# Layer 2 of a four-layer gated model, rebuilt: exponential ahead of the clip, packed normalise, shorter output product, work shared out anew over VectorE, ScalarE, GpSimd and TensorE

## The reference, cut to what matters

```python
x = x + tanh(g_xattn[2]) * L2_xattn(layernorm(x), ctx, mask, ...)
x = x + tanh(g_ffn[2]) * L2_ffn(layernorm(x), w_gate, w_up, w_down)

# L2_xattn: 16 heads of 16 columns
q, k, v = proj(hs, Wq, bq), proj(at, Wk, bk), proj(at, Wv, bv)
scores = clip(einsum(q, k) / 4, -50, 50)
scores = clip(where(attend, scores, -10000.0), -50, 50)
probs = softmax(scores); probs = probs / (probs.sum(-1) + 1e-8)
delta = (probs @ v) @ Wo.T + bo
delta = clip(residual_scale, 0, 0.3) * delta
delta = (delta - mean) / sqrt(var + 1e-5) * ln_gamma + ln_beta

# L2_ffn: 832 hidden columns
weight_quant(w) = clip(round(w * s), -1, 1) / s           # s = 1 / mean|w|
act_quant(x)    = clip(round(x * s), -128, 127) / s       # s = 127 / max|x| of the row
bitlinear(x, w) = act_quant(x) @ weight_quant(w).T
y = bitlinear(silu(bitlinear(x, w_gate)) * bitlinear(x, w_up), w_down)
```

## Time and profile before

| | us |
|---|---|
| median of 3 runs | 2442.97 (2437.24 to 2443.68) |
| the profiled execution | 2458.33 |
| its span | 2456.8 |
| layer 2 in it: from 1261.34 to 1675.53 | 414.2 |
| VectorE busy in the span | 1617.9 (66%) |
| TensorE busy in the span | 1959.7 (80%) |

### The profile page before, as it was taken

The page is one execution under the profiler, slowest core; times in us unless marked ns, Lnnn a source line. Parts: engine busy times, 40 slices in busy tenths (PEclk is TensorE's granted clock), DMA queues, the critical chain, the costliest instruction groups (busy, mean ns, idle before and its releaser), DMA issues.

```text
span 2456.8 us, 35107 instructions
## 1 busy us (share of the span) xinstructions
PE 1959.7 (80%) x12408; PEld 1268.5 (52%) x12438; DVE 1617.9 (66%) x3820; ACT 900.5 (37%) x2036; POOL 526.9 (21%) x623
## 2 busy tenths in 40 slices
PE   6888899999976888787864655545699999987697
PEld 2444445555545667675233433323466666656344
DVE  8888744544358999998247777772356666655447
ACT  3666621111114656665122333321234334433232
POOL 3122100000012333332112222111013322332231
PEclk8999999999997999999886777776899999998869
DMA  4543120000014333331112332206100000000966
GB/s 96 155 99 67 39 84 0 1 1 0 1 23 91 77 72 72 77 75 32 46 30 78 91 88 59 52 1 224 60 1 29 29 14 6 1 1 1 249 194 259
DMA packets 160397, 158.03 MB, mean 64 GB/s; under 512 B 84424, under 2 KB 139088, under 8 KB 156288
## 3 DMA queue, kind: packets, MB, share of 16 engines
q1 hardware_dynamic: 150912, 146.31, 22.4%
q0 software_dynamic: 6144, 8.82, 1.1%
q10 hardware_dynamic: 3168, 0.66, 0.1%
HBM read 103.27 MB, written 60.82 MB: 67 GB/s over the span
## 4 chain that ended last, share of the span: by engine, by line
PE 53%; DVE 31%; issue 8%; ACT 5%; DMA 2%; POOL 1%; SPq 0%; ACTq 0%; another core or an unknown queue 0%; DVEq 0%; POOLq 0%
PE psum L983 10%; PE psum L1003 5%; PE psum L2857 4%; PE psum L2783 4%; DVE sbuf L534 3%; PE psum L381 3%; PE psum L1891 2%; DVE sbuf L1539 2%; PE psum L2850 2%; DVE sbuf L1546 2%; PE psum L2832 2%; PE psum L344 2%; PE psum L2819 1%; DVE sbuf L2348 1%; PE psum L3348 1%
## 5 line engine op out<-in xcount | busy, mean ns | idle before, releaser
L983 PE MATMUL psum<-sbuf 128*128 128x512 f32 (+1 forms) x544 | 246.7, 596 | 0.0
L181 POOL TENSOR_TENSOR sbuf<-sbuf 128x1 f32<-128x1 f32 x128 | 73.9, 580 | 747.7 <-DVE sbuf L173 747.1
L534 DVE TENSOR_REDUCE sbuf<-psum 128x2 f32<-128x512 f32 x256 | 164.8, 685 | 30.5 <-PE psum L344 29.4
L3170 ACT ACTIVATE sbuf<-psum,sbuf 128x128 f32<-128x128 f32 x256 | 113.8, 454 | 188.2 <-DVE sbuf L3005 182.2
L1677 ACT ACTIVATE sbuf<-psum 128x512 f32<-128x512 f32 x256 | 139.9, 597 | 107.5 <-PE psum L1403 94.3
L1109 DVE SCALAR_TENSOR_TENSOR sbuf<-sbuf,psum 128x512 f32<-128x512 f32 (+1 forms) x68 | 46.8, 688 | 196.8 <-ACT sbuf L1172 196.8
L983 PEld LDWEIGHTS psum<-sbuf 128*128 128x128 f32 (+1 forms) x544 | 100.4, 188 | 106.6 <-issue 104.2
L1172 ACT ACTIVATE sbuf<-psum 128x512 f32<-128x512 f32 (+1 forms) x68 | 40.7, 598 | 310.0 <-PE psum L983 310.0
L681 ACT ACTIVATE sbuf<-psum 128x1024 f32<-128x1024 f32 x128 | 130.7, 1023 | 41.5 <-PE psum L366 34.5
L1003 PE MATMUL psum<-sbuf 128*128 128x256 f32 (+1 forms) x544 | 129.2, 380 | 0.7 <-DVE sbuf L1114 0.7
L2783 PE MATMUL psum<-sbuf 128*128 128x256 f32 x512 | 123.0, 396 | 3.4 <-DVE sbuf L2963 1.9
(11 more groups left out here) (388 smaller groups left out, 4555.7 us busy)
## 6 DMA issues: line engine op xcount, KB each, us to landing
l_pair_outputs<-sbuf SPq DMA_DIRECT2D x24, 512.0 KB, 6.9
sbuf<-in_l_gu_pairs SPq DMA_DIRECT2D x32, 384.0 KB, 8.9
sbuf<-l_pair_outputs SPq DMA_DIRECT2D x16, 768.0 KB, 15.1
sbuf<-l_q_parts SPq DMA_DIRECT2D x16, 384.0 KB
l_q_parts<-sbuf SPq DMA_DIRECT2D x64, 96.0 KB, 2.0
sbuf<-l_q_parts SPq DMA_DIRECT2D x32, 192.0 KB
l_k_parts<-sbuf SPq DMA_DIRECT2D x64, 96.0 KB, 2.0
sbuf<-l_k_parts SPq DMA_DIRECT2D x32, 192.0 KB
```

The costliest lines, as they stand in the source:

```text
L534: dve.tensor_reduce(top3[:, 2 * hp:2 * hp + 2, c], score_bank[v % 2].rearrange("p (j t) -> p j t", j=2), AXX, ALU.max, negate=True).then_i ...
L983: last = pe.matmul(up_bank[v % 2][0:M, n * BANK:(n + 1) * BANK], wn[:, k, fs], xt_t[blk % 2][:, k, :], start=(k == 0), stop=(k == KD - 1))
L3170: last = act.activation(e_t[u % 3][:, j * P:(j + 1) * P], score_bank[:, j * P:(j + 1) * P], ACT.Exp, bias=mt[:, j:j + 1], scale=rq[:, lo + ...
```

## The change

Attention. `act_exp` now reads the scores from PSUM and writes SBUF, and `dve_clip` clips the exponentials in place, in SBUF, between exp(50) and exp(-50). `dve_normalise` writes only the 16 used columns of each head (128 in place of 256), so its second turn, the stored tile and Wo halve: `pe_project_out` has two products, and a third one of a single row (ones times `row`), which brings in both biases: `row` is bv through Wo plus bo, made once by `pe_bias_row`. Wo is scaled by the residual scale once, gamma and beta by the gate, all in `act_scale_weights`. The sums of the norm are taken from PSUM (`dve_delta_stats`), `dve_add_attention` is two instructions, and beta is added to x ahead, by `pool_add_beta`. The bias of keys and queries and the copy of values move from VectorE to ScalarE (`act_bias`, `act_values`), and the norm ahead of the queries to GpSimd (`pool_norm`).

Feed-forward. The mean is taken off on ScalarE (`act_less_mean`), 1/sqrt(var) enters only as a factor of the scale, the rounded values are turned as fp32 (`m.ident` in place of `m.ident_bf`) and lose ROUND in the copy out of PSUM, so `act_xq` and `act_hq` go. Three scales of a block move to GpSimd (`pool_scales`, `pool_out_scale`). `hq_bank` is now banks 6 and 7, `down_bank` 5.

The loop has 19 passes (NB + 3): attention of block i, whose second half is weighed and normalised in pass i + 1, norm and quantising of block y = i - 2, gate and down product of block f = i - 3. The order in each pass is new on all engines. The clearing of Wo (L2020, a memset on VectorE at the start of layer 1's feed-forward part) goes.

```diff
     def load(self):
-        dve.wait_ge(*self.m.x_l1a.at(NB))
-        dve.memset(self.wo, 0.0).then_inc(*self.cleared.up())
...
     def pe_project_out(b):
         pe.wait_ge(*normed.at(2 * b + 2))
-        for j in range(4):
-            last = pe.matmul(av_bank[:, 0:D], attn_t[b % 2][:, j * P:(j + 1) * P], w.wo[:, j, :], start=(j == 0), stop=(j == 3))
+        pe.wait_ge(*av_read.at(min(2 * b + 3, 2 * NB)))
...
+        pe.matmul(av_bank[:, 0:D], ones[0:1, :], row, start=True, stop=False)
+        for s in range(2):
+            last = pe.matmul(av_bank[:, 0:D], attn_t[b % 2][:, s * P:(s + 1) * P], w.wo[:, s, :], start=False, stop=(s == 1))
...
-        dve.tensor_scalar(d_t[u % 4], score_bank, 50.0, -50.0, ALU.min, ALU.max).then_inc(*clipped.up())
+        dve.wait_ge(*exped.at(u + 1))
+        dve.tensor_scalar(d_t[u % 4], d_t[u % 4], EXP_HIGH, EXP_LOW, ALU.min, ALU.max).then_inc(*clipped.up())
...
-        dve.tensor_tensor(T3, T3, R.unsqueeze(2).broadcast_to([P, 8, 32]), ALU.mult).then_inc(*m.chain.up())
+        dve.tensor_tensor(packed.rearrange("p (c j r) -> p j c r", j=2, r=HD2), T3[:, :, :, 0:HD2],
+                          R.rearrange("p (j c) -> p j c", j=2).unsqueeze(3).broadcast_to([P, 2, 4, HD2]), ALU.mult).then_inc(*m.chain.up())
...
     def dve_add_attention(b):
+        dve.scalar_tensor_tensor(d, av_bank[:, 0:D], s[:, 6:7], w.gamma, ALU.subtract, ALU.mult).then_inc(*y_read.up())
+        dve.wait_ge(*y_rstd.at(b + 1))
+        dve.wait_ge(*beta_added.at(b + 1))
+        dve.wait_ge(*y_read.at(b + 1))
+        dve.scalar_tensor_tensor(m.X[b], d, s[:, 8:9], m.X[b], ALU.mult, ALU.add).then_inc(*x_mid.up())
...
+    def act_less_mean(f):
+        act.wait_ge(*f_var.at(f + 1))
...
+        act.activation(n_t[f % 2], m.X[f], ACT.Identity, bias=ffn_stats[f % 2][:, 6:7], scale=-1.0).then_inc(*f_less.up())
...
     def pe_turn_hq(f):
-        pe.wait_ge(*hq_ready.at(f + 1))
+        pe.wait_ge(*h_round.at(f + 1))
...
+    def pool_norm(pair):
...
+            pool.wait_ge(*rstd_ready.at(n + 1))
+            pool.tensor_scalar(xn[:, i * D:(i + 1) * D], m.X[n], s[:, 6:7], s[:, 8:9], ALU.subtract, ALU.mult).then_inc(*xn_ready.up())
+
+    def pool_add_beta(b):
+        pool.wait_ge(*xn_ready.at(b + 1))
+        pool.tensor_tensor(m.X[b], m.X[b], w.beta, ALU.add).then_inc(*beta_added.up())
...
     def pool_program():
...
+        for i in range(NB + 3):
+            f, y, j, pair = i - 3, i - 2, made_in(i), i // 2 + 2
+            if 0 <= y < NB:
+                pool_delta_root(y)
             if j < 2 * NPAIR:
                 pool_rest(j)
                 pool_lo(j)
+            if f >= 0:
+                pool_out_scale(f)
+            if 0 <= y < NB:
+                ln_root(m, y, f_var, f_rstd, ffn_stats)
+            if 0 <= y < NB:
+                pool_scales(y)
...
     def act_program():
+        for i in range(NB + 3):
+            f, y, j = i - 3, i - 2, made_in(i)
+            if i < NB:
+                act_exp(2 * i)
+            if j < 2 * NPAIR:
+                act_bias(j)
+                act_hi(j)
+            if i < NB:
+                act_exp(2 * i + 1)
+            if i % 2 == 1 and j < 2 * NPAIR:
+                act_keep_x(i // 2 + 2)
+            if j < 2 * NPAIR:
+                act_mid(j)
+            if 0 <= y < NB:
+                act_less_mean(y)
+            if f >= 0:
+                act_keep_hq(f)
+            if i + 2 < NB:
+                act_values(i + 2)
+            if 0 <= y < NB:
+                act_keep_xq(y)
+                act_tanh(y)
```

More of the change, by code:

```diff
@@ L2031, in load @@
         sp.dma_start(self.mask, A["mask2T"]).then_inc(*loaded.up(16))
-        sp.wait_ge(*self.cleared.now())
-        wo = A["l2_woT"].rearrange("(j q d) o -> q d j o", q=4, d=HD2)
-        for q in range(4):
-            sp.dma_start(self.wo[32 * q:32 * q + HD2], wo[q]).then_inc(*loaded.up(16))
 class L3Weights:
@@ L2231, in pe_add_sums @@
         pe.wait_ge(*sums_ready.at(1))
-        pe.matmul(g_bank[:, 0:4], ones, wsum[:, 0:4], start=True, stop=True).then_inc(*sums_added.up())
+        pe.matmul(sums_bank[:, 0:4], ones, wsum[:, 0:4], start=True, stop=True).then_inc(*sums_added.up())
     def pe_program():
@@ L2494, in dve_program, with act_scale_weights, act_bias, act_keep_row @@
                 dve.wait_ge(*weights_ready.at(4))
-            if b < NB:
-                dve_normalise(b, 1)
-            if f >= 0:
-                dve_ffn_add(f)
-            if 1 <= b <= NB:
-                dve_ffn_quantise(b - 1)
+            if 1 <= i <= NB:
+                dve_delta_stats(i - 1)
+    def act_scale_weights():
+        act.wait_ge(*w.loaded.now())
+        act.activation(w.gamma, w.gamma, ACT.Copy, scale=m.gates[:, 2:3]).then_inc(*scaled.up())
+        act.activation(w.beta, w.beta, ACT.Copy, scale=m.gates[:, 2:3]).then_inc(*scaled.up())
+        act.activation(w.bq, w.bq, ACT.Copy, scale=0.25).then_inc(*scaled.up())
+        act.wait_ge(*set_ready.at(1))
+        act.activation(w.wo, w.wo, ACT.Copy, scale=w.rs).then_inc(*scaled.up())
+    def act_bias(j):
+        pair, i = divmod(j, 2)
+        made, bias, scale, bank_read = ((k_made, w.bk, 1.0, k_read), (q_made, w.bq, 0.25, q_read))[i]
+        val = val_t[j % 2][:, 0:KD * N]
+        act.wait_ge(*made.at(pair + 1))
+        if j == 1:
+            act.wait_ge(*scaled.at(3))
+        if j >= 2:
+            act.wait_ge(*p_lo.at(j - 1))
+        for c in range(KD):
+            last = act.activation(val[:, c * N:(c + 1) * N], pro_bank[:, c * N:(c + 1) * N], ACT.Identity, bias=bias[:, c:c + 1], scale=scale)
+        last.then_inc(*bank_read.up())
+    def act_keep_row():
+        act.wait_ge(*row_made.at(1))
+        act.activation(row, row_bank[0:1, 0:D], ACT.Copy).then_inc(*row_kept.up())
     def act_keep_x(pair):
@@ L2547, in act_keep_hq @@
     def act_keep_hq(f):
-        pb, full = hq_bank.bitcast(BF16), (NF2 - 1) * P
+        full = (NF2 - 1) * P
         act.wait_ge(*hq_turned.at(f + 1))
@@ L2555, in act_program @@
     def act_program():
         act.wait_ge(*m.x_l1f.at(NBLK))
-        act.wait_ge(*set_ready.at(4))
+        act_scale_weights()
+        act_bias(0)
         act_keep_x(0)
         act_hi(0)
+        act_bias(1)
+        act_hi(1)
         act_mid(0)
-        act_hi(1)
+        act_bias(2)
+        act_keep_x(1)
         act_mid(1)
-        act_keep_x(1)
         act_hi(2)
+        act.wait_ge(*cleared.now())
+        act_values(0)
+        act_values(1)
+        act_keep_row()
         act_mid(2)
-        for b in range(NB + 2):
-            f = b - 2
-            if f >= 0:
-                act_keep_xq(f)
-            if b < NB:
-                act_exp(b, 0)
-            j = 2 * (b // 2 + 1) + 1 if b % 2 == 0 else 2 * (b // 2 + 2)
+        act.wait_ge(*set_ready.at(4))
@@ L2581, in act_program @@
-            if b % 2 == 1 and b // 2 + 2 < NPAIR:
-                act_keep_x(b // 2 + 2)
+            if 0 <= y < NB:
+                act_less_mean(y)
             if f >= 0:
-                act_hq(f)
                 act_keep_hq(f)
-            if 1 <= b <= NB:
-                act_xq(b - 1)
+            if i + 2 < NB:
+                act_values(i + 2)
+            if 0 <= y < NB:
+                act_keep_xq(y)
+                act_tanh(y)
+    def pool_norm(pair):
+        if pair:
+            pool.wait_ge(*xn_turned.at(pair))
+        for i in range(PAIR):
+            n = PAIR * pair + i
+            s = pro_stats[n % len(pro_stats)]
+            pool.wait_ge(*rstd_ready.at(n + 1))
+            pool.tensor_scalar(xn[:, i * D:(i + 1) * D], m.X[n], s[:, 6:7], s[:, 8:9], ALU.subtract, ALU.mult).then_inc(*xn_ready.up())
@@ L2615, in pool_program @@
             ln_root(m, n, var_ready, rstd_ready, pro_stats)
-        for j in range(3):
-            pool_rest(j)
-            pool_lo(j)
-        for b in range(NB + 2):
-            j = 2 * (b // 2 + 1) + 1 if b % 2 == 0 else 2 * (b // 2 + 2)
-            if 1 <= b <= NB:
-                pool_delta_root(b - 1)
+        pool_norm(0)
+        pool_rest(0)
+        pool_norm(1)
+        pool_lo(0)
+        pool_rest(1)
+        pool_lo(1)
+        pool.wait_ge(*scaled.at(2))
+        for b in range(4):
+            pool_add_beta(b)
+        pool_rest(2)
+        pool_lo(2)
+        for i in range(NB + 3):
+            f, y, j, pair = i - 3, i - 2, made_in(i), i // 2 + 2
+            if 0 <= y < NB:
+                pool_delta_root(y)
             if j < 2 * NPAIR:
```

372 lines of the change are left out of this document (166 added, 206 removed).

## The result

The changed kernel takes 2374.91 us (median, 2371.20 to 2378.24) where the kernel before takes 2443.17 (2437.24 to 2443.68): a ratio of 0.972, 95% interval 0.969 to 0.975. Run again on another chip, beside experiments 7 and 10, it gave 0.968 (0.965 to 0.971). It saves 68 us; the forecast was 88 us, so the time is 20 us above the predicted 2355 and inside the range.

What follows compares the result with a forecast made beforehand. VectorE, with waits on top, was taken to bound the kernel before. A new pass of 15.2 + 1.2 + 0.6 = 17.0 us gave layer 2 327 against 414.2; with the memset, 2443.0 becomes 2355 us, range 2322 to 2395.

Steps and rivals of the forecast that it cites:

- What bounded the kernel before: Layer 2's long stretch: VectorE's work, about 18.6 us a pass, plus waits of about 3.7; new VectorE floor 13.6.
- The ring: One new pass walked gate to gate through VectorE, ScalarE and TensorE: about 14.7 us, 15.2 with VectorE's queue.
- The sum: Layer 2: head 34.1, passes 0 to 2 36, thirteen passes at 17.0 us 221, tail 36; together 327 us.
- The clock: TensorE's products at the lower clock after idle stretches: 1.2 us a pass charged, of 5 if all ran there.
- VectorE's queue: VectorE's own order holds the up product back by 0 to 0.8 us in passes with sums for a pair.
- The rival that the lower clock rules: TensorE's lower clock sets the passes: 19.3 us a pass, tail 40, kernel 2389 us; 20 in 100.
- The tail: Layer 2's last three passes, by the same ring with what work is left: 14.3, 12.7 and 8.9, 36 us.
- The collision: VectorE against GpSimd around the gate's rounding and the second add of attention: one wait of 0.6 us a pass.
- The output product: TensorE's step on the ring after the up product: three products of the same form instead of four, 1.5 us.
- Passes 0 to 2: Layer 2's first passes, with weight rounding in passes 0 and 1 and no gate in pass 2: 36 us.
- GpSimd's norm: Norm ahead of the queries, moved to GpSimd: 0.73 us an instruction taken, between bounds of 0.73 and 44 us.
- Slower than before: Rival: a costly `pool_norm` on GpSimd, no gain from 16 us a norm, 2800 us at 44; 4 in 100.

Runs made afterwards that it cites:

- experiment 7: The changed kernel with the norm ahead of the queries back on VectorE, at the end of every even pass: 0.970 of the kernel before.
- experiment 10: The kernel of experiment 9 with four extra TensorE products, results unused, ahead of the turn of the gated rows: 0.956 of the kernel before.
- experiment 6: The kernel before with its 32 clips left out, the exponential reading the scores from PSUM: 0.983 of the kernel before.
- experiment 5: The changed kernel with all 32 clips of the exponentials left out: 0.969 of the kernel before.
- experiment 1: The changed kernel with two ScalarE steps exchanged, `act_keep_hq` ahead of `act_less_mean`: 0.961 of the kernel before.
- experiment 8: The changed kernel with a fourth product added to the output product, its result written over: 0.978 of the kernel before.
- Experiment 2: The changed kernel with unused TensorE products, five ahead of the turn of the gated rows and four ahead of the down product: 0.963 of the kernel before.
- experiment 3: The changed kernel with `pool_lo` moved behind GpSimd's root, no longer beside VectorE's second add of attention: 0.966 of the kernel before.
- experiment 9: The changed kernel with the orders of experiment 1 and experiment 3, plus VectorE's sums of the output product behind the gate: 0.954, 2333.5 us.

## Why the prediction came out as it did

**What bounded the kernel before**, VectorE with waits on top, fits experiment 6, which does not separate it from the shorter chain; experiment 5 shows that VectorE's work does not bound the changed kernel. Its floor was 13.6 us a pass, and it is busy 13.1 (170.33 / 13).

**The ring** was right as a mechanism and in its order. Gate, `less_mean` with `keep_hq`, and the sums at the end hold to 0.1 us; experiment 1 confirms that ScalarE's order puts the sums on it, experiment 8 that the output product is on it. The wait at `dve_delta_stats` is 2.1 us (1 to 3 forecast), TensorE's wait ahead of the turn 2.5 (2 to 3), ScalarE's work 7.3 us a pass (7 to 8).

**The sum** missed by 19.5 us, all in layer 2: head 34.1 and 34.1, passes 0 to 2 39.1 (36 forecast), thirteen passes 231.6 (221), tail 41.8 (36): 0 + 3.1 + 10.6 + 5.8.

**The clock, the term that was too small.** 1.2 us a pass were charged. By the table, down, values, turn, weighing and up take 6.75 us where 4.65 were counted: 2.1 us more. Experiment 2, which gave 1.7 us of them back by putting products in the waits, shows the cause. The rest may be VectorE's queue, for which 0.5 us had been put on apart; no run shows it. The wrong step was to read from the one up product of 1.57 us in the earlier trace rows that the clock would be back for the larger part of the ring. It is back for the output product, and for up in most passes, but down and values follow the waits, and they ran at the lower rate in nearly every pass of the changed kernel (down in twelve of thirteen, values in all eleven). The clock is the largest term missed. The pass of 17.8 us lies within the forecast's 15.8 to 18.4 all the same.

The rival that the lower clock rules (19.3 us a pass, 2389) is 1.5 us a pass above the measured 17.8, where the forecast is 0.8 below; by the time of the kernel it is nearer, 14 us above where the forecast is 20 below, because it had the longer tail as well. Its 19.3 does not hold the whole 5 us: with 5 us in place of 1.2 the prediction's own sum is 20.8 a pass. That is too much, since up is at 1.5 in seven of the thirteen passes. The Trainium skill's page "TensorE: Matmul & The Clock Gate", section "HAM oscillation — how this bites in real kernels", describes a loop whose waits of 3 to 5 us bring the array back to the lower clock each time. The waits here are shorter, 2.5 and 2.0 us on average and 3.1 at most, so the page does not speak of quite this case, and the 2404 that the prediction drew from it is 29 us too high. In its direction the trace agrees: the products behind the waits ran at the lower clock, the granted clock was 0.77, and 0.95 with fillers in the waits.

**The tail** has the same term in it. With less work between its waits TensorE has a granted clock of 0.59 there, its product up takes 2.96 us and the wait ahead of each turn 5.5. The forecast had it on the ring with the mixed price; the three passes took 16.7, 15.1 and 10.0 us. In experiment 2 the fillers took 2.7 of the 5.8 us back (the tail is 39.0 us there); for the rest the clock is an explanation that no run shows.

**The collision** was right in kind and place: the second add of attention beside `pool_lo`. 0.6 us was charged and it is 0.6 on average over the thirteen passes (1.09 against 0.48 us, experiment 3). The same step, add and sums, was counted 0.3 us too short besides: it takes 2.0 without any collision.

**The output product** was counted as three of the four products, 1.5 us. It is 1.79: the two full ones (L2197) take 1.13 us where 1.0 was counted, and the third, one row deep, that brings in both biases (L2195) takes 0.69 us where a third of the 1.5 had been put on it.

Added up: +0.1 gate, +0.9 add and sums, +2.1 clock, +0.3 output product are 3.4 above the 14.7 us of the walk; 2.3 had been put on it (0.5 for the queue, 1.2, 0.6). That is 18.1 us for a pass with values; two of the thirteen have none, hence the mean of 17.8.

**Passes 0 to 2** took 3.1 us more. The rows show waits that the walk did not have, the longest of 5.11 us at the turn of x for GpSimd's norm; but with the norm on VectorE (experiment 7) this stretch is 2.2 us longer still, so the norm is not shown to be the cause. It stays open.

**GpSimd's norm** costs 1.2 to 1.3 us in ten of its sixteen instructions, 1.7 to 2.4 in the others, and not 0.73; what holds the longer ones is not shown. The bounds were right, the choice in them wrong, and in the passes it did not matter (experiment 7). GpSimd was busy 32% of the passes, where some 40% were foreseen. **The clip** is 0.68 us (0.74 forecast), **the halved instructions** of `dve_normalise` 0.30 and 0.31 (0.3), and seven fp32 turns take 1.15 us in the pass shown beside 1.07 for bf16 ones in the earlier trace rows, nearly the same, as assumed. VectorE was busy 73.5% with 33 instructions a pass, just under the 75% and the 34 to 37 that were listed. The longer pass explains the share; the number of instructions was counted slightly too high.

**Slower than before** needed a norm on GpSimd of over 16 us. It is 1.5 on average in the passes.

## What to carry over

When the engine that bounds a loop is relieved, look at what stands ahead of each step of the new ring in its engine's queue: here three changes of order (experiments 1, 3 and 9), with no work taken away, were worth 36 us in layer 2, more than half of what the whole rebuild had brought. Where TensorE's granted clock is low before a change and waits remain in the new pass, charge the products that follow a wait at the lower clock, one by one, and only those further on at the higher, in place of a share of the total. And take gains that lie on one path once: two edits that gave 1.5 and 0.7 us alone gave 1.5 together. Before waits are filled to raise the clock, look which slow product stands behind which wait: experiment 10 filled the wrong one.
